# Gate rows laid over partitions by two DMAs per chunk, and the output matrix folded into the values, in a gated cross-attention block with 32 experts

## The reference

```python
x = x + tanh(g_xattn) * xattn(ctx_768, layernorm(x), mask, ...)      # x: 4 x 256 x 128, ctx: 4 x 256 x 96
x = x + tanh(g_ffn) * ffn(layernorm(x), expert_sel, keys, values)

# xattn: 2 heads of 64; keys and values from 256 context rows and 256 latent rows
q = ln @ Wq.T
kv = concatenate([xn @ Wkv.T, ln @ Wlkv.T], axis=1)
attn = softmax(where(mask, rmsnorm(q) * SCALE @ rmsnorm(k).T, -max))
out = (attn @ v) @ Wo.T + bo

# ffn: 32 experts of 64 hidden values, 4 of them chosen for each token
gates = sigmoid(einsum('nd,ed->ne', xt, expert_sel))
gate_full = gates where among the 4 largest of the token, else 0
scores = relu(einsum('nd,edf->nef', xt, keys)) * gate_full[:, :, None]
out = einsum('nef,efv->nv', scores, values)
```

## Time and profile before

| | us |
|---|---|
| median of 3 runs | 139.21 (139.10 to 139.27) |
| profiled execution | 139.16 |
| its span, first to last instruction | 137.4 |
| TensorE busy | 117.6 (86%), 616 matmul records |
| VectorE busy | 108.7 (79%) |
| ScalarE busy | 82.4 (60%) |
| GpSimd busy | 18.6 (14%) |
| mean granted TensorE clock | 0.959 of full |

### The profile page before, as it was taken

The page is one execution under the profiler, slowest core; times in us unless marked ns, Lnnn a source line. Parts: engine busy times, 40 slices in busy tenths (PEclk is TensorE's granted clock), DMA queues, the critical chain, the costliest instruction groups (busy, mean ns, idle before and its releaser), DMA issues.

```text
span 137.4 us, 2089 instructions
## 1 busy us (share of the span) xinstructions
PE 117.6 (86%) x616; PEld 81.3 (59%) x616; DVE 108.7 (79%) x333; ACT 82.4 (60%) x188; POOL 18.6 (14%) x43
## 2 busy tenths in 40 slices
PE   5917955696879799799896999999998999999990
PEld 5904534353646497378673676667766667767760
DVE  5877699887979959698496699998994799769852
ACT  5214698749893255337546756764575687587720
POOL 4050000700012493000330000004040000000000
PEclk9995599959999999999999999999999999999998
DMA  4699000000000000000000000000000000000004
GB/s 87 203 366 389 12 2 0 0 2 0 5 0 0 0 0 5 2 0 0 0 5 0 0 0 0 0 2 0 0 0 7 0 0 0 0 0 0 2 5 153
DMA packets 2171, 4.28 MB, mean 31 GB/s; under 512 B 240, under 2 KB 1648, under 8 KB 1904
## 3 DMA queue, kind: packets, MB, share of 16 engines
q1 hardware_dynamic: 2160, 4.15, 8.7%
HBM read 3.63 MB, written 0.52 MB: 30 GB/s over the span
## 4 chain that ended last, share of the span: by engine, by line
PE 65%; DVE 18%; ACT 6%; issue 6%; POOL 1%; POOLq 1%; DVEq 0%; ACTq 0%
PE bank L717 10%; PE bank L719 9%; PE bank L718 9%; PE bank L818 9%; PE bank L873 5%; PE bank L746 4%; PE bank L750 3%; PE bank L828 3%; PE bank L773 3%; PE bank L801 2%; DVE keys L542 2%; PE bank L803 2%; PE bank L807 1%; PE bank L805 1%; DVE shift_l L365 1%
## 5 line engine op out<-in xcount | busy, mean ns | idle before, releaser
L542 DVE TENSOR_TENSOR keys<-bank,values 128x512 f32<-128x512 f32 x32 | 21.9, 689 | 7.6 <-ACT values L686 6.4
L686 ACT ACTIVATE values<-bank 128x512 f32<-128x512 f32 x32 | 19.1, 596 | 12.8 <-PE bank L719 12.8
L550 DVE TENSOR_TENSOR hid_lo<-keys,hid_hi 128x512 fp32r<-128x512 f32 x32 | 21.2, 683 | 0.8 <-ACT hid_hi L693 0.4
L693 ACT ACTIVATE hid_hi<-keys 128x512 fp32r<-128x512 f32 x32 | 19.6, 628 | 2.5 <-PE bank L719 1.6
L717 PE MATMUL bank<-hid_hi,v_lo 128*128 128x512 f32 x32 | 16.2, 506 | 0.0
L818 PE MATMUL bank<-prob,proj 128*65 128x256 f32 x64 | 15.1, 382 | 0.2 <-ACT prob L647 0.2
L717 PE MATMUL bank<-xm_hi,k_lo 128*128 128x512 f32 x32 | 14.6, 455 | 0.6 <-ACT gateT L677 0.6
L647 ACT ACTIVATE prob<-bank 128x512 f32<-128x512 f32 x16 | 8.9, 594 | 9.4 <-PE bank L807 7.8
L873 PE MATMUL bank<-gateT,expand 96*128 96x512 bf16 x32 | 12.5, 391 | 0.9 <-DVE keys L542 0.8
L719 PE MATMUL bank<-hid_hi,v_hi 128*128 128x512 f32 x32 | 12.7, 396 | 0.0
L718 PE MATMUL bank<-xm_lo,k_hi 128*128 128x512 f32 x32 | 12.6, 395 | 0.0
(11 more groups left out here) (134 smaller groups left out, 248.7 us busy)
## 6 DMA issues: line engine op xcount, KB each, us to landing
keys<-keys_in SPq DMA_DIRECT2D x1, 1024.0 KB, 7.8
values<-values_in SPq DMA_DIRECT2D x1, 1024.0 KB, 9.8
out<-x_mid SPq DMA_DIRECT2D x4, 128.0 KB, 1.9
wa<-wa_in SPq DMA_DIRECT2D x1, 320.0 KB, 3.6
vecs_x<-x_in SPq DMA_DIRECT2D x1, 256.0 KB, 5.5
cx<-ctx_in SPq DMA_DIRECT2D x2, 96.0 KB, 2.8
cx<-ctx_in SPq DMA_DIRECT2D x1, 192.0 KB, 5.9
wb<-wb_in SPq DMA_DIRECT2D x1, 145.0 KB, 5.8
```

What stands on the lines that cost most here:

```text
L542: dve.tensor_tensor(hid[:, n % 3, :], gates_bank(n)[:, :], relu[:, n % 2, :], ALU.mult).then_inc(hid_ready, 1)
L550: dve.tensor_tensor(hid_lo[:, n % RING, :], hid[:, n % 3, :], hid_hi[:, n % RING, :].bitcast(F32), ALU.subtract).then_inc(hid_lo_ready, 1)
L686: act.activation(relu[:, n % 2, :], bank[H_BANK[n % 2]][:, :], ACT.Relu).then_inc(relu_ready, 1)
L693: act.activation(hid_hi[:, n % RING, :], hid[:, n % 3, :], ACT.Copy).then_inc(hid_hi_ready, 1)
```

## The change

The diff does these things.

1. *Gates by DMA.* `gateT` is now f32, 32 rows (one for each expert) x tokens, turned straight from `gate`; the three bf16 parts, `expand` and its product in `up` are gone. SP issues two DMAs for each chunk, each reading one row of `gateT` (one partition, 512 tokens, 2 KB) as 64 copies into 64 partitions of a slot of `gated`. There are six slots; SP waits until the chunk six before is used.
2. *relu in the product.* VectorE's `up` reads the hidden values from PSUM, takes the larger of them and 0 and multiplies by `gated` in one scalar_tensor_tensor; ScalarE's relu is gone, and `H_BANK` has three banks.
3. *First chunks whole.* The first eight chunks go down in one f32 product with unsplit `hid` and `values`.
4. *Output matrix folded.* `fold` multiplies the output matrix into the value weights once; `vlat` and `vctx` make, for each batch, values of 128 columns and head from it, `project` makes only queries and keys. `attend` now has `prob` as the stationary side and gives output rows at once; `out_proj` on TensorE, `oT` and `proj` are gone (VectorE's stage `out_proj` is kept).
5. *Result turned.* `x_mid` is turned (`turn_res`) and the result is added and stored as 128 x 1024, VectorE reading the accumulator itself; the array is turned back outside.
6. *Constants and orders.* VectorE's memsets go to GpSimd and ScalarE but for one; warm-up products are spread over the start; GpSimd's `low_parts` wait for `max_done`; `wb` is loaded earlier; all three orders are written anew.

The core of it (the orders, the start of `turn_in`, and host arrays are left out):

```diff
-WARM_UP = 12
-DOWN = 3
-RING = DOWN + 1
+WARM_UP = 1
+RING = 4
+WHOLE = 8
-G = 6
+SLOTS = 6
...
-        gateT = sb("gateT", [3 * E, B, S], BF16)
-
-        relu = values[:, 0:2 * HN].rearrange("p (i n) -> p i n", i=2)
+        gateT = sb("gateT", [E, B, S])
+
+        gated = inT[:, :, :, :].rearrange("p i b s -> p (i b s)").rearrange("p (i n) -> p i n", i=SLOTS)
...
+            for h in range(HALF):
+                sp.wait_ge(gateT_ready, HB * (h + 1))
+                for c in range(EC):
+                    n = EC * h + c
+                    if n == 0:
+                        sp.wait_ge(proj_done, 2 * B)
+                        sp.wait_ge(vlat_done, B)
+                        sp.wait_ge(vctx_done, B)
+                    if n >= SLOTS:
+                        sp.wait_ge(hid_ready, n - SLOTS + 1)
+                    for i in range(2):
+                        row = gateT[2 * c + i:2 * c + i + 1, HB * h:HB * h + HB, :].rearrange("p b s -> p (b s)")
+                        sp.dma_start(gated[F * i:F * i + F, n % SLOTS, :],
+                                     row.unsqueeze(1).to_broadcast([1, F, HN])).then_inc(gated_in[n % SLOTS], 16)
...
-                dve.wait_ge(relu_ready, n + 1)
-                dve.wait_ge(spread_done, n + 1)
-                if n >= 3:
-                    dve.wait_ge(hid_hi_ready, n - 2)
-                    dve.wait_ge(hid_lo_ready, n - 2)
-                dve.tensor_tensor(hid[:, n % 3, :], gates_bank(n)[:, :], relu[:, n % 2, :], ALU.mult).then_inc(hid_ready, 1)
+                dve.wait_ge(up_done, n + 1)
+                dve.wait_ge(gated_in[n % SLOTS], 32 * (n // SLOTS + 1))
+                free_hid(n - 3)
+                dve.scalar_tensor_tensor(hid[:, n % 3, :], bank[H_BANK[n % len(H_BANK)]][:, :], 0.0, gated[:, n % SLOTS, :],
+                                         ALU.max, ALU.mult).then_inc(hid_ready, 1)
...
-                pe.matmul(gates_bank(n)[:, :], expand[:, cc], half(gateT, h), start=True, stop=True).then_inc(spread_done, 1)
...
+                if n < WHOLE:
+                    pe.wait_ge(hid_ready, n + 1)
+                    last = pe.matmul(bank[ACC_BANK[h]][:, :], values[:, cc], hid[:, n % 3, :],
+                                     start=(c == 0), stop=(c == EC - 1))
...
+            def fold(i):
+                pe.wait_ge(wo_ready, 1)
+                for a in range(HEADS):
+                    wo = wb[:, B_WO + D * a:B_WO + D * a + D]
+                    pe.matmul(bank[7][:, D * a:D * a + D], wb[:, B_LV + D * a:B_LV + D * a + D], wo, start=True, stop=True)
+                    last = pe.matmul(bank[7][0:DC + 1, D * (HEADS + a):D * (HEADS + a) + D],
+                                     wb[:, B_CV + (DC + 1) * a:B_CV + (DC + 1) * (a + 1)], wo, start=True, stop=True)
+                last.then_inc(fold_done, 1)
...
+                for a in range(HEADS):
+                    for j in range(KT):
+                        last = pe.matmul(bank_of(b, OUT + t)[:, WOA * a:WOA * a + WOA], prob[:, b % 2, a, j, P * t:P * t + P],
+                                         vw[:, b, j, a, :], start=(j == 0), stop=(j == KT - 1))
                 last.then_inc(attend_done, 1)
```

More of the change, by code:

```diff
@@ L69 @@
+    turn_res 2, up 1.13, up 1.14, up 1.15, down 1.9, down 1.10, down 1.11, down 1.12, down 1.13, down 1.14,
+    down 1.15, turn_res 3
 """
 DVE_ORDER = """
[L71 to L74, removed]
@@ L107 @@
[L107 removed]
+B_LV, B_CV = 0, HEADS * D
+B_WO = B_CV + HEADS * (DC + 1)
+B_ONE = B_WO + HEADS * D
+B_COLS = B_ONE + P
 def stages(order):
@@ L719, in product, with warm @@
                 return pe.matmul(o, lh, rh, start=False, stop=stop)
+            def warm(i):
+                if i == 0:
+                    pe.wait_ge(ident_ready, 1)
+                for _ in range(WARM_UP):
+                    pe.matmul(bank[5][:, 0:P], ident[:, :], ident[:, :], start=True, stop=True)
             def turn_in(b):
-                if b == 0:
-                    pe.wait_ge(ident_ready, 1)
-                    for _ in range(WARM_UP):
-                        pe.matmul(bank[7][:, 0:P], ident[:, :], ident[:, :], start=True, stop=True)
                 bk = bank_of(b, TURN_IN)
+                if b == 3:
+                    pe.wait_ge(vlat_ready, HB)
                 pe.wait_ge(xn_ready, KT * b + BT)
@@ L754, in turn_qk @@
-            def turn_qk(b):
-                pe.wait_ge(proj_ready, 3 * (b + 1))
-                for kind, tiles, first in ((0, KT, 0), (1, BT, KT)):
-                    pe.wait_ge(qk_ready, 2 * b + kind + 1)
-                    for t in range(tiles):
-                        src = qk[:, b, HEADS * (first + t):HEADS * (first + t + 1), :].rearrange("p a d -> p (a d)")
-                        last = pe.transpose(bank_of(b, TURN_QK + kind)[:, P * t:P * t + P], src, ident[:, :])
-                    last.then_inc(qkT_done, 1)
+                pe.wait_ge(inT_ready, 2 * b + 1)
@@ new lines, in project @@
+                if b >= HB:
+                    pe.wait_ge(vlat_ready, b + 1)
+                for t in range(BT):
+                    last = pe.matmul(bank_of(b, PROJECT)[:, 4 * DH * t:4 * DH * (t + 1)], xnT[:, b, P * t:P * t + P],
+                                     wa[:, A_LAT:A_CTX], start=True, stop=True)
+                last.then_inc(proj_done, 1)
+                pe.wait_ge(inT_ready, 2 * b + 2)
+                if b >= HB:
+                    pe.wait_ge(vctx_ready, b + 1)
+                for t in range(BT):
+                    last = pe.matmul(bank_of(b, PROJECT + 1)[:, P * t:P * t + P], cnT[0:DC, b, P * t:P * t + P],
+                                     wa[0:DC, A_CTX:A_SEL], start=True, stop=True)
@@ new lines, in vlat @@
+            def vlat(b):
+                pe.wait_ge(fold_ready, 2)
+                pe.wait_ge(inT_ready, 2 * b + 1)
+                if b == 1:
+                    pe.wait_ge(vlat_ready, 1)
+                if b == 3:
+                    pe.wait_ge(vctx_ready, HB)
+                bk = value_bank(b, 0)
+                for t in range(BT):
+                    lat = xnT[:, b, P * t:P * t + P]
+                    for a in range(HEADS):
+                        o = bk[:, D * (HEADS * t + a):D * (HEADS * t + a) + D]
+                        last = pe.matmul(o, lat, folded[:, D * a:D * a + D], start=True, stop=(a > 0))
+                        if a == 0:
+                            pe.matmul(o, wb[:, B_ONE:B_ONE + P], wb[:, B_WO:B_WO + D], start=False, stop=True)
+                last.then_inc(vlat_done, 1)
@@ new lines, in vctx @@
+            def vctx(b):
+                if b == 0:
+                    pe.wait_ge(row_ready, 1)
+                if b == 1:
+                    pe.wait_ge(vctx_ready, 1)
+                pe.wait_ge(fold_ready, 2)
+                pe.wait_ge(inT_ready, 2 * b + 2)
+                bk = value_bank(b, 1)
+                for t in range(BT):
+                    last = pe.matmul(bk[:, HEADS * D * t:HEADS * D * (t + 1)], cnT[:, b, P * t:P * t + P],
+                                     folded[0:DC + 1, HEADS * D:], start=True, stop=True)
+                last.then_inc(vctx_done, 1)
@@ new lines, in turn_qk @@
+            def turn_qk(b):
+                pe.wait_ge(qk_ready, 2 * b + 1)
+                for t in range(BT):
+                    src = qk[:, b, 4 * t:4 * t + HEADS, :].rearrange("p a d -> p (a d)")
+                    last = pe.transpose(bank_of(b, TURN_QK + 1)[:, P * t:P * t + P], src, ident[:, :])
+                last.then_inc(qkT_done, 1)
+                pe.wait_ge(qk_ready, 2 * b + 2)
+                for t in range(KT):
+                    first = KT * HEADS + HEADS * t if t < BT else 4 * (t - BT) + HEADS
+                    src = qk[:, b, first:first + HEADS, :].rearrange("p a d -> p (a d)")
+                    last = pe.transpose(bank_of(b, TURN_QK)[:, P * t:P * t + P], src, ident[:, :])
+                last.then_inc(qkT_done, 1)
@@ new lines, in down, with turn_res @@
+                last.then_inc(down_done, 1)
+            def turn_res(b):
+                pe.wait_ge(mid_ready, BT * (b + 1))
+                if b == 1:
+                    pe.wait_ge(gateT_ready, HB + 1)
+                else:
+                    pe.wait_ge(logit_ready, HB + 1 if b != 2 else B)
+                if b == 3:
+                    pe.wait_ge(midT_ready, 1)
+                for t in range(BT):
+                    last = pe.transpose(res_bank(b)[:, P * t:P * t + P], x_mid[:, BT * b + t, :], ident[:, :])
+                last.then_inc(midT_done, 1)
@@ L897, in _ @@
+            run = {"warm": warm, "turn_in": turn_in, "project": project, "turn_qk": turn_qk, "row_max": row_max, "turn_max": turn_max,
+                   "weights": lambda at: weights(*at), "fold": fold, "vlat": vlat, "vctx": vctx, "attend": lambda at: attend(*at),
                    "turn_mid": turn_mid, "select": select, "turn_gates": turn_gates,
-                   "up": lambda at: up(*at), "down": lambda at: down(*at), "finish": finish}
```

(1 more changed line is left out.)

443 lines of the change are left out of this document (197 added, 246 removed).

## The result

| | before | changed |
|---|---|---|
| median, us | 139.24 (139.1 to 141.39, 4 runs) | 343.06 (340.76 to 343.36, 4 runs) |
| ratio | | 2.461, 95% interval 2.4477 to 2.4743 |
| profiled execution, its span, us | 139.16, 137.4 | 343.36, 341.6 |
| TensorE / VectorE / ScalarE busy, us | 117.6 / 108.7 / 82.4 | 157.3 / 102.7 / 58.4 |
| mean granted TensorE clock | 0.959 | 0.655 |

The ratio compares the means of the runs and leaves out the 141.39 us of before, a run in a slower state.

The account below looks back on a forecast made before the run. TensorE bounds the expert stage before; afterwards gate transfers from one partition would. Gates ready 68, first landing 1.3, 32 x 9.8 = 314, last chunk 6.0: 389 us of span, 390 us forecast, range 225 to 430 at 80 in 100.

Parts of the forecast that it names:

- main case: Expert chunks: gates take 9.6 to 11 us a chunk, ready at 66 to 73 us; 375 to 430 us, 71 in 100.
- rival with two rows at once: Gate transfers: reads of both rows overlap at 26.7 GB/s each, 4.9 us a chunk, 234 us; 9 in 100.
- Start: Kernel start: VectorE's constants mostly go, first statistics near 3 us, context next late; about 2.2 us gained.
- Gates ready: End of attention and gates stage: first half's gates ready between 66 and 73 us, taken as 68.
- The product: VectorE's product of gates and hidden values, relu included, from PSUM: 0.738 instead of 0.689 us.
- A chunk's gates: Two gate transfers a chunk, one behind the other in the same queue: 9.8 us a chunk, 314 us for 32.
- The upper end as the value to take: Rate of a one-partition source: one engine's share, 26.7 GB/s, chosen over 427 GB/s, since each partition had one packet a transfer.
- First landing: First gate transfer: lands 1.3 us more than its own transfer time (1.9 less 0.6).
- After the last product: End of kernel: the last chunk, from its product through down passes and result to the store, 6.0 us.
- SP is no limit: SP's DMA issues: one follows the other after 0.43 us, 0.86 us a chunk.
- Clock: TensorE in the waits: falls to half clock, 2.8 us a chunk, covered by 9.8.
- Rival with a free source: Read side: one partition keeps up from 175 GB/s on, gates hidden in 0.61 us; 127 us (122 to 133), 16 in 100.

Follow-up runs that it names:

- e6: Changed kernel with the two gate rows of a chunk on partitions c and 32 + c: 369.24 us.
- e2: Changed kernel with the turned gates four partitions apart (expert e on partition 4e): 219.76 us.
- e5: Changed kernel with one DMA a chunk instead of two, neighbouring rows outermost, so that two engines carry it: 383.21 us.
- e9: Changed kernel with the splits of chunks 13 and 14 of the second half moved before the product of chunk 15: 341.79 us.
- e1: Changed kernel with each transfer reading 64 partitions of x instead of one gate row (result of no use): 122.94 us, 0.889 of before.
- e4: Changed kernel with the turned gates of each half stored once to HBM and the copies read from there: 123.97 us, 0.891 of before.
- e8: Changed kernel with one DMA a chunk carried by two engines and the gate rows four partitions apart: 241.89 us.
- e7: Changed kernel with the two gate rows of a chunk on partitions c and 64 + c: 232.54 us.

## Why the prediction was right, and where its terms were off

The direction and the mechanism held: the chunks wait for gates that come out of one place at 27 GB/s. Forecast 390 us, range 225 to 430, measured 343.06. The main case, 375 to 430 us at 71 in 100, was missed: the result lies between it and the rival with two rows at once (234 us), and the range holds it since it was drawn to cover both. By the steps of the prediction:

- *Start.* Right. First statistics at 3.04 us (5.83 before), next late the context at 3.73 us, as worked out from the earlier trace rows.
- *Gates ready.* Forecast 68, measured 65.98 + 0.37 = 66.35 us. The added products for the values didn't make that later than forecast.
- *The product.* Forecast 0.738 us, measured 0.692; the relu inside it cost nothing against the earlier trace rows.
- *A chunk's gates.* This is the term that was mis-sized: 9.8 us forecast, 8.20 measured. 31 x 1.6 = 50 us less; the gates ready, the first landing and the end give -1.7, +1.1 and +2.7, together the 47 us between forecast and result. The rate of one place was right: 26 to 28 GB/s in the plateaus, 9.78 us in e6, where the place stays the same. The step that failed is "the two rows don't help each other much: their transfers stand one behind the other in the same queue", taken to hold for all transfers. It holds inside four partitions; when a transfer for the next four follows, the rate goes to 47 GB/s, as it would with packets of both in flight, and two chunks take 16.4 us in place of 19.6. With a border at every transfer (e2) a chunk takes (208.71 - 73.73) / 31 = 4.35 us, more than two full shares (60 GB/s).
- *The upper end as the value to take.* Right, and for the reason given only in part: I argued that no partition ever gave more than one engine's rate. But those rows had one engine to a partition throughout (and even that from 2160 / 15 packets, a mean), so they couldn't tell a limit of the engine from one of the place; that the place gives to sixteen engines just what one engine moved, 26.8 beside 26.7 GB/s, was luck as far as the rows go. e2 and e5 show that the sharing is wider than a partition. The sentence on the ports of the Trainium skill was the better description; from the rows of before alone neighbouring rows might have overlapped.
- *First landing.* From the gates to the first product 78.51 - 66.35 = 12.2 us, forecast 9.8 + 1.3. The 1.3 was summed wrongly: it takes 0.6 us, the time of a whole chunk at 427 GB/s, off the landing of a store of 128 KB, whose own time would be 0.3; 1.6 would be right, and a little nearer.
- *After the last product.* Forecast 6.0 us, measured 8.7. The prediction counted one chunk; VectorE's order has two splits, and so TensorE two more chunks, behind the product that waits; moving the splits ahead (e9) took off 1.3 of the 2.7 us. It should have asked what is queued behind a new wait at the end of the order.
- *SP is no limit.* Right in effect, but the issues don't take 0.43 us: SP's rows show up to 5.00 us for one, median 4.758, and 12% of the chain. SP is held up by the transfers, not the other way round: the issues of as many DMAs take 2.106 us at the median in e2 and 0.597 in e1, so they follow the speed of the source. That a full queue holds SP is the likely way, which no view shows.
- *Clock.* Fell as forecast, 0.57 in the stage, and is covered: at half clock a chunk's passes (2.8 us) are far under 8.2 us.
- *Rival with a free source.* Priced at 127 us. With the source out of the way e1 takes 122.94 and e4 123.97 us, so the price of everything else was 3 to 4 us too high, and nearly all of it is the gates: in e1 they are ready at 64.02 + 0.37 = 64.39 us, 3.6 before the forecast. From there to the end of the span it is 121.1 - 64.39 = 56.7 us, priced at 52.9 + 4.2 = 57.1. So the change holds two parts of opposite sign: the rest of it takes some 16 us off (139.37 before, beside e1's 122.94), and reading one SBUF row 64 times puts 220 us on.
- *Rival with two rows at once.* 4.9 us a chunk and 234 us were its price; e8, which makes it true, took 5.12 us a chunk and 241.89 us.

What stays open: how these 16 us divide between folding, unsplit first chunks, the relu and the orders; no run takes them apart.

## What to carry to other kernels

Before a broadcast by DMA is written, work out the rate that its source must give, not only that of the transfer: here 175 GB/s from four partitions that give 27. Here it paid to read the copies from HBM (e4, 173 GB/s with 3.5 us of waiting in all). To lay the rows so that successive transfers read partitions four or 64 apart brought a chunk from 8.20 to 4.35 and 4.71 us, three times what the other engines need. And a DMA share near one with few GB/s in the profile's slices was the sign of such a place; the share alone looks like a full DMA, and with two engines (e5) it was 0.12 at hardly fewer GB/s.

## What the runs showed that I had not expected

- Overlap at a change of place gives more than two shares: 60 GB/s in e2, against 51 for two engines on two such places (e8), and e7 has 53 to 54 while two places take turns and 58 to 60 where a third follows. That fits packets of a third transfer in flight; no view shows the packets themselves.
- A kernel that is 2.5 times slower differs from one that is 11% faster than before only in where the copies are read, with one store of the gates for each half: 343.06 and 123.97 us.
- SP's issue of a DMA isn't a fixed price: 0.43 us in the loads, 0.6 us at the median in e1 and e4, 2.1 in e2 and 4.8 in the changed kernel.
